# Plain float32 products in the expert layer of a fused attention and mixture-of-experts kernel

## The reference

```python
x  = L0_attn_x
xn = layernorm(x)
out = x + attention(xn, w_qkv, w_out) + ffn(xn, wg, w1, b1, w2, b2)

def ffn(...):                      # 8 experts, 2 of them for each token
    xt = xn.reshape(8192, 256)
    scores = softmax(xt @ wg); topv, topi = top_k(scores, 2)
    # each expert takes 2048 tokens (capacity), others are dropped
    disp = zeros(8, 2048, 256) with the chosen tokens' rows at their slots
    h = relu(einsum("ecm,emh->ech", disp, w1) + b1)     # w1: 8 x 256 x 1024
    y = einsum("ech,ehm->ecm", h, w2) + b2              # w2: 8 x 1024 x 256
    out = sum over the 2 choices of gate * y[expert, slot]
```

## Time and profile before

| | |
|---|---|
| median of the runs | 3241.0 us |
| time of the profiled execution | 3247.3 us |
| its span on the core | 3245.3 us |
| TensorE busy | 3037.0 us, 94% |
| TensorE weight loads busy | 2426.4 us |
| VectorE busy | 2254.5 us, 69% |
| ScalarE busy | 1674.7 us, 52% |
| GpSimd busy | 1612.6 us, 50% |

### The profile page before, as it was taken

How to read it: one execution, slowest core, us unless ns; L and a number is a source line. 1 busy time by engine, 2 the same in 40 slices (tenths; PEclk the granted TensorE clock), 3 DMA queues, 4 the chain that set the end, 5 groups by cost and what they waited for, 6 DMA issues and landing times.

```text
span 3245.3 us, 64713 instructions
## 1 busy us (share of the span) xinstructions
PE 3037.0 (94%) x22677; PEld 2426.4 (75%) x22677; DVE 2254.5 (69%) x5152; ACT 1674.7 (52%) x3798; POOL 1612.6 (50%) x2384
## 2 busy tenths in 40 slices
PE   5589999999989999999999999999999999999996
PEld 3479998999977777777777777777777777777774
DVE  6844444444347778778877877787788778777875
ACT  2444444444445555555555555555555555555553
POOL 2132221222136665666566566656665665666563
PEclk7799999999999999999999999999999999999999
DMA  6022221222123323333233333333332333333232
GB/s 207 32 78 75 72 72 56 65 74 77 51 63 78 96 76 100 89 87 105 73 100 78 100 80 94 100 79 92 85 100 73 100 97 84 83 90 98 70 90 71
DMA packets 205201, 274.70 MB, mean 85 GB/s; under 512 B 61520, under 2 KB 161872, under 8 KB 204896
## 3 DMA queue, kind: packets, MB, share of 16 engines
q1 hardware_dynamic: 180288, 203.51, 22.6%
q0 software_dynamic: 24608, 67.17, 7.7%
HBM read 102.80 MB, written 33.55 MB: 42 GB/s over the span
## 4 chain that ended last, share of the span: by engine, by line
PE 55%; ACT 6%; DVE 5%; issue 4%; SPq 1%; DMA 0%; DVEq 0%
PE S L1272 14%; PE O L1309 13%; PE S L1188 8%; PE T L1285 8%; ACT pr L1347 4%; PE W L1223 3%; PE S L1203 3%; PE W L1203 3%; PE W L1188 3%; DVE pr L1404 2%; DVE kl L1435 1%; ACT kh L1362 1%; DVE ol L1449 1%; SPq L1125 1%; ACT oh L1372 1%
## 5 line engine op out<-in xcount | busy, mean ns | idle before, releaser
L1347 ACT ACTIVATE pr<-pr,negm 128x128 f32<-128x128 f32 (+7 forms) x1024 | 787.2, 770 | 756.5 <-DVE negm L1404 755.3
L1549 POOL TENSOR_SCALAR pr<-pr,rinv 128x128 f32<-128x128 f32 (+7 forms) x1024 | 759.6, 749 | 828.8 <-DVE rinv L1410 821.4
L1404 DVE CUSTOM_DVE_ANT_0 pr<-S,late 128x128 f32<-128x128 f32 (+7 forms) x1024 | 731.0, 751 | 48.1 <-PE S L1272 40.5
L1309 PE MATMUL O<-pT,vv 128*64 128x256 f32 (+1 forms) x5120 | 558.0, 364 | 14.0 <-DMA pT<-squares 13.2
L1309 PEld LDWEIGHTS O<-pT,vv 128*64 128x64 f32 x5120 | 345.7, 137 | 203.8 <-issue 24.1
L1339 DVE COPY pT<-T 128x512 f32<-128x512 f32 (+3 forms) x704 | 364.1, 540 | 147.3 <-PE O L1309 147.3
L1285 PE MATMUL T<-ident,pr 128*128 128x128 f32 x2688 | 420.6, 281 | 19.2 <-DVE pT L1339 18.6
L886 DVE TENSOR_TENSOR hl<-h,hh 128x512 fp32r<-128x512 f32 x256 | 191.5, 748 | 317.7 <-ACT hh L847 310.6
L1285 PEld LDWEIGHTS T<-ident,pr 128*128 128x128 f32 x2688 | 295.8, 140 | 133.5 <-issue 95.5
L843 ACT ACTIVATE h<-pH,b1c 128x512 f32<-128x512 f32 x256 | 175.9, 687 | 366.9 <-PE pH L773 353.0
L1272 PE MATMUL S<-kh,qh 64*128 64x512 f32 (+2 forms) x1536 | 319.6, 407 | 39.0 <-DVE negm L1404 34.9
(11 more groups left out here) (186 smaller groups left out, 6543.5 us busy)
## 6 DMA issues: line engine op xcount, KB each, us to landing
pT<-squares SPq DMA_DIRECT2D x768, 128.0 KB
pT<-squares POOLq DMA_DIRECT2D x256, 128.0 KB
y<-yb SPq DMA_DIRECT2D x128, 128.0 KB, 1.7
wr<-in_L_attn_w_qkv SPq DMA_DIRECT2D x128, 128.0 KB, 2.3
x<-in_L_attn_x SPq DMA_DIRECT2D x16, 512.0 KB, 5.4
xn<-xn SPq DMA_DIRECT2D x16, 512.0 KB, 5.1
w1r<-in_L_ffn_w SPq DMA_DIRECT2D x8, 1024.0 KB
w2r<-in_L_ffn_w SPq DMA_DIRECT2D x8, 1024.0 KB
```

Of the source, the lines that this page charges most:

```text
L1309: ins = e.matmul(O[hs, a:GQ], vv[n // 2 % 2][:, kt, vs], turned_p, start=(kt == 0), stop=(kt == KT - 1))
L1347: e.activation(pr[i][:, 0:w], pr[i][:, 0:w], ACT.Exp, bias=negm[:, i:i + 1], scale=-1.0, accum_out=rsum[:, i:i + 1]).then_inc(expd.sem, 1)
L1404: e.tensor_tensor_reduce(pr[i][:, 0:w], S[s % 2][:, off:off + w], late[:, SEQ - w:], 1.0, -MASKED, ALU.add, ALU.min, negm[:, i:i + 1]).the ...
L1549: e.tensor_scalar(pr[i][:, 0:width(s)], pr[i][:, 0:width(s)], rinv[:, i:i + 1], 1.0, ALU.mult, ALU.mult).then_inc(scaled.sem, 1)
```

## The change

The experts' tiles become plain float32: `xT` in place of `xh` and `xl`, `w1` and `w2` (two buffers each, which the DMA fills) in place of raw, high and low parts, `hT` in place of `h`, `hh` and `hl`. Each product of both projections is one `matmul` of float32 tiles in place of three of float32r tiles. The row copies move from ScalarE to VectorE, ScalarE writes `hT` straight from `pH`, all splitting of weights goes. SyncE now issues the loads of an expert's weights after the four stores of the group, not before them. The buffers `yb` move to an allocation that lasts over the next stage.

```diff
 def route(...):
             e.activation(ex[:]...., w[:]...., ACT.Exp).then_inc(s_exp, 1)
-            round_first(e)
             e.wait_ge(s_iota, 2)
...
 def experts(...):
-        xh = two(lambda i: sb(f"xh{i}", [P, MC, GS], F32R))
-        xl = two(lambda i: sb(f"xl{i}", [P, MC, GS], F32R))
+        xT = two(lambda i: sb(f"xT{i}", [P, MC, GS]))
...
-        h32 = two(lambda i: sb(f"h32_{i}", [P, GS]))
-        hh = two(lambda i: sb(f"hh{i}", [P, HC, GS], F32R))
-        hl = two(lambda i: sb(f"hl{i}", [P, HC, GS], F32R))
-        yb = [sb(f"yb{i}", [P, MODEL]) for i in range(GT)]
+        hT = two(lambda i: sb(f"hT{i}", [P, HC, GS]))
+        yb = start_of_next.yb
...
         @block.sync
-                        if g == 0 and not (last and par == 1):
-                            e.wait_ge(wlo.sem, wlo.at(x, 2))
-                            if first and par == 0:
...
-                            load_w(x + 1, 1 - par)
...
                             e.dma_start(row(yv_d, ...), yb[t][:]).then_inc(yst[t].sem, 16)
+
+                        if g == 0 and not (last and par == 1):
+                            apart(e, s_apart[1])
+                            load_w(x + 1, 1 - par)
...
         @block.gpsimd
-                        if g == 1 and not (last and par == 1):
-                            e.wait_ge(fY.sem, fY.at(sg - 1, 0))
-                            split(x + 1, 1 - par)
...
         @block.tensor
             def up(sg, par, q, hc, first):
                 if hc == 0:
-                    e.wait_ge(xhi.sem, xhi.at(sg, 1))
-                    e.wait_ge(xlo.sem, xlo.at(sg, 1))
+                    e.wait_ge(xt.sem, xt.at(sg, 1))
...
-                terms = [(w1h, xh), (w1h, xl), (w1l, xh)]
-                n = 0
                 for m in range(MC):
-                    for w, xx in terms:
-                        ins = e.matmul(pH[hc % 4][:], w[par][:, m, ws], xx[q][:, m, :], start=(n == 0), stop=(n == 3 * MC - 1))
-                        n += 1
+                    ins = e.matmul(pH[hc % 4][:], w1[par][:, m, ws], xT[q][:, m, :], start=(m == 0), stop=(m == MC - 1))
                 ins.then_inc(fH.sem, 1)
 
             def down(sg, par, q, t, first):
                 if t == 0:
-                    e.wait_ge(hlo.sem, hlo.at(sg, HC))
+                    e.wait_ge(rl.sem, rl.at(sg, HC))
...
                 for hc in range(HC):
-                    for n, (hs, ws) in enumerate(((hh, w2h), (hh, w2l), (hl, w2h))):
-                        ins = e.matmul(pY[t % 2][:], hs[q][:, hc, ts_], ws[par][:, hc, :],
-                                       start=(hc == 0 and n == 0), stop=(hc == HC - 1 and n == 2))
+                    ins = e.matmul(pY[t % 2][:], hT[q][:, hc, ts_], w2[par][:, hc, :], start=(hc == 0), stop=(hc == HC - 1))
...
         @block.scalar
-                            e.activation(h32[hc % 2][:], pH[hc % 4][:], ACT.Relu, bias=b1c[par][:, hc:hc + 1]).then_inc(rl.sem, 1)
...
-                            e.activation(hh[q][:, hc, :], h32[hc % 2][:], ACT.Copy).then_inc(hhi.sem, 1)
...
+                            e.activation(hT[q][:, hc, :], pH[hc % 4][:], ACT.Relu, bias=b1c[par][:, hc:hc + 1]).then_inc(rl.sem, 1)
...
         @block.vector
             def rows(sg, q, first=False):
+                e.wait_ge(tX.sem, tX.at(sg, 1))
+                if not first:
+                    e.wait_ge(fH.sem, fH.at(sg - 2, HC))
                 for m in range(MC):
-                    ins = e.tensor_tensor(xl[q][:, m, :], pX[m][:], xh[q][:, m, :].bitcast(F32), ALU.subtract)
-                ins.then_inc(xlo.sem, 1)
+                    ins = e.tensor_copy(xT[q][:, m, :], pX[m][:])
+                ins.then_inc(xt.sem, 1)
...
-                            e.tensor_tensor(hl[q][:, hc, :], h32[hc % 2][:], hh[q][:, hc, :].bitcast(F32),
-                                            ALU.subtract).then_inc(hlo.sem, 1)
```

More of the change, by code:

```diff
@@ L323, in _, with route @@
             turn(UNITS - 1, 1, False)
-def route(nc, k, logits, pick, slot_token, prefetch, biases, round_first):
+def route(nc, k, logits, pick, slot_token, prefetch, biases):
     E = EXPERTS
@@ L541, in biases @@
                              bass.IndirectOffsetOnAxis(ap=t["rows"][0:EXPERTS * HC, 0:1], axis=0)).then_inc(t["s_b1"], 16)
-    return t, first, biases, round_first
+    return t, first, biases
 class Start:
@@ L573, in __init__ @@
         self.s_xn = [sem(f"s_start_xn{i}") for i in range(len(self.pr))]
+        self.yb = [sb(f"yb{i}", [P, MODEL]) for i in range(4)]
         self.s_yst = [sem(f"s_yst{i}") for i in range(4)]
@@ L680, in body @@
                         sg, q = PER * x + g, g % 2
-                        if g == 0 and not (last and par == 1):
-                            e.wait_ge(wlo.sem, wlo.at(x, 2))
-                            if first and par == 0:
+                        if first and par == 0 and g == 0:
+                            for b in range(2):
                                 apart(e, s_apart[1])
[L685 to L692, removed]
+                                e.wait_ge(gat[b].sem, gat[b].at(0, 16 * GT))
                             apart(e, s_apart[1])
-                            load_w(x + 1, 1 - par)
+                            e.wait_ge(fH.sem, fH.at(0, 1))
                         if last and par == 1 and g == 1:
@@ L723, in gather @@
                                          bass.IndirectOffsetOnAxis(ap=idx[q][:, t:t + 1], axis=0)).then_inc(gat[q].sem, 16)
[L725 to L730, removed]
             gather(0, 0, 0, True)
@@ L754, in rows @@
                 if not first:
[L755 to L756 removed]
+                    e.wait_ge(xt.sem, xt.at(sg - 1, 1))
                 for m in range(MC):
@@ L817, in _ @@
         def _(e):
[L818 to L824, removed]
             e.wait_ge(s_b1t, 1)
             e.activation(b1T[:], pY[0][:, 0:EXPERTS * HC], ACT.Copy).then_inc(s_b1c0, 1)
-            rows(0, 0, True)
             def body(i, first, last):
@@ L837, in body @@
                         sg, q = PER * x + g, g % 2
-                        start = first and par == 0 and g == 0
                         for hc in range(HC):
                             e.wait_ge(fH.sem, fH.at(sg, hc + 1))
-                            if not (start and hc < 2):
-                                e.wait_ge(hlo.sem, hlo.at(sg, hc - 1))
-                            e.activation(h32[hc % 2][:], pH[hc % 4][:], ACT.Relu, bias=b1c[par][:, hc:hc + 1]).then_inc(rl.sem, 1)
-                            e.wait_ge(rl.sem, rl.at(sg, hc + 1))
                             if hc == 0 and not (first and par == 0 and g < 2):
                                 e.wait_ge(fY.sem, fY.at(sg - 2, GT))
-                            e.activation(hh[q][:, hc, :], h32[hc % 2][:], ACT.Copy).then_inc(hhi.sem, 1)
-                            if hc == 2 and not (last and par == 1 and g == PER - 1):
-                                rows(sg + 1, (g + 1) % 2, start)
+                            e.activation(hT[q][:, hc, :], pH[hc % 4][:], ACT.Relu, bias=b1c[par][:, hc:hc + 1]).then_inc(rl.sem, 1)
             loop(e, body)
@@ L854, in _, with rows @@
         def _(e):
-            def rows(sg, q):
-                e.wait_ge(xhi.sem, xhi.at(sg, 1))
+            def rows(sg, q, first=False):
+                e.wait_ge(tX.sem, tX.at(sg, 1))
+                if not first:
+                    e.wait_ge(fH.sem, fH.at(sg - 2, HC))
                 for m in range(MC):
-                    ins = e.tensor_tensor(xl[q][:, m, :], pX[m][:], xh[q][:, m, :].bitcast(F32), ALU.subtract)
-                ins.then_inc(xlo.sem, 1)
-            def split(x, q, j):
-                raw, hi, lo = ((w1r, w1h[q], w1l[q]), (w2r, w2h[q], w2l[q]))[j]
-                e.wait_ge(whi.sem, whi.at(x, j + 1))
-                e.tensor_tensor(lo[:], raw[:], hi[:].bitcast(F32), ALU.subtract).then_inc(wlo.sem, 1)
+                    ins = e.tensor_copy(xT[q][:, m, :], pX[m][:])
+                ins.then_inc(xt.sem, 1)
             def down(sg, par, t, first):
@@ L872, in down @@
                 e.tensor_tensor(yb[t][:], pY[t % 2][:], b2c[par][:], ALU.add).then_inc(yv.sem, 1)
-            split(0, 0, 0)
-            split(0, 0, 1)
-            rows(0, 0)
+            rows(0, 0, True)
             def body(i, first, last):
@@ L884, in body @@
                         for hc in range(HC):
-                            e.wait_ge(hhi.sem, hhi.at(sg, hc + 1))
-                            e.tensor_tensor(hl[q][:, hc, :], h32[hc % 2][:], hh[q][:, hc, :].bitcast(F32),
-                                            ALU.subtract).then_inc(hlo.sem, 1)
                             if hc == 2 and not (last and par == 1 and g == PER - 1):
-                                rows(sg + 1, (g + 1) % 2)
+                                rows(sg + 1, (g + 1) % 2, start)
                             if hc % 2 and not start:
```

(4 more changed lines are left out.)

42 lines of the change are left out of this document (15 added, 27 removed).

## The result

The changed kernel takes 3403.43 us (median of two runs, 3402.16 to 3404.69), against 3241.0 before: ratio 1.0501 with a 95% interval of 1.0456 to 1.0546. It is 5.0% slower, 162 us. The forecast was 3398 us in a range of 3385 to 3460 us. The profiled execution took 3402.2 us with a span of 3400.3.

The account below looks back on a forecast made before the run. TensorE's product time was taken to bound the experts' stage; products +160.7, start -1.1 and stall -2.8 us summed to +156.8 us on the median of 3241.0, giving 3398 us, range 3385 to 3460 us.

Parts of the forecast that it names:

- What bounds: Experts' products stretch, 752.6 us: only TensorE's product time counts; less work on other engines is worth nothing except where TensorE waited.
- Price of a float32 record: Experts' products: each float32 product is two records, 0.427 us each for 512 columns, 0.217 for 256; +160.7 us.
- The upper bound from the whole round: One attention round of float32 products, start and handover included: at most 0.227 us for a record of 256 columns.
- Products before: Experts' float32r products in the kernel before: 1536 x 0.232 plus 3072 x 0.1188, 721 us in all.
- The second way to 721: Experts' stretch of 752.6 us less 4.4 us of standing still and 27 us of transposes leaves 721 us.
- The stall: TensorE's 2.8 us wait before the first down product goes, as the split and `hl` go: -2.8 us.
- Start: Start of the experts' stage: rows go through VectorE alone, first product 1.1 us earlier; between 0 and -2 us.
- The split of the first weights: VectorE's work at the stage's start, said to be hidden by the 10.7 us wait for the gather: gives nothing.
- The first: Rival: in the experts' stage a float32 product costs only two float32r products, 481 us replacing 721; 2997 us, chance 0.03.
- the rule of the Trainium skill: Matrix engine peak "÷2 for FP32_LOW_HIGH": for the whole product a gain, for each of two records in agreement with the trace.
- The second rival: Experts' float32 products keep float32r's pace for each column pass, 0.464 us per 512-column record; 3478 us, chance 0.06.
- The third and fourth: Rivals: tiles go through as one float32r record, 2757 us, chance 0.01; TensorE waits once a group, 3430 us, chance 0.05.

Follow-up runs that it names:

- the two halves of the change: The kernel before with only the up products in plain float32, ratio 1.0258, and with only the down products in plain float32, ratio 1.0247.
- The experiment with the later rounding: The kernel before, with GpSimd's rounding of an expert's weights waiting for one down tile more: 3238.11 us, ratio 0.9987.
- The idle subtractions: The kernel after the change with two idle 128 x 2048 subtractions on VectorE at the start of the experts' stage: 3403.24 us.

## Why the prediction was right

- **What bounds.** Shown. With 218 us less of VectorE's work and 188 us less of ScalarE's in the stretch, the time followed TensorE's products alone, and the two halves of the change added up.
- **Price of a float32 record.** 0.427 us was taken, 0.4288 measured for 512 columns; 0.217 taken, 0.2156 measured for 256. The attention's 0.2156 us is the very number of the new down products: whether 64 columns of weights or 128 makes no difference. Up 437 forecast and 439 measured, down 444 and 442, together 881.6 and 881. The upper bound from the whole round, 0.227 us, was not reached in any group; that a start and a handover made it so is argued, not shown.
- **Products before.** 721 us was 4 us too much. Its paces come from one of the dearest groups; on the mean of eight, (23.27 - 0.88) x 32 = 717 us. The second way to 721 agreed only because it left out that TensorE ran at a granted clock of 0.50 (the 1.2 GHz level) from 169.6 to 173.4 us and from 190.5 to 193.5, which cost 1.8 and 1.4 us. So the products grew by 164 us, not by 160.7.
- **The stall.** The 2.8 us went as forecast, and 1.4 us at the lower clock behind it went too, which the prediction did not count. The experiment with the later rounding shows both. A wait of 1.9 us for issue stands in place of 1.6. The first twelve records took 7.84 us (162.98 to 170.82) in place of 5.1, which is 0.9 us more lost at the lower clock than at the same place before. Together: 164 - 2.8 - 1.4 + 0.3 + 0.9 = 161 us, by which the stretch grew; 157.9 were forecast for it.
- **Start.** -1.1 us for the row copies, as forecast. The split of the first weights was put at nothing, since the wait for the gather covered it. That step was wrong, by 3.0 us: the cover was itself lengthened by the work that it was to hide. The idle subtractions gave back 1.7 of them through the gathers, the one subtraction left in each half of the change 1.8, mostly through the copy. The 2.5 us ahead of the stage are chance.
- **The number.** 3398 forecast, 3403 measured. The two profiled executions differ by 154.9 us, 2 less than the forecast 156.8, the medians by 162.4: the profiled execution of before lay 6 us over its median. That the sum comes within 2 us is partly luck, since 5.5 us too little were taken off at the start (3.0 and 2.5) and 3 us too little were put on in the stretch of the products. The price of the float32 records, which makes the loss, does not hang on this.
- **Rivals.** The first (a float32 product at the price of two float32r ones) needed a record of 256 columns under 0.178 us; full weights and one product at a time give 0.2156. There were two ways to read the rule of the Trainium skill, Perfetto Trace Analysis, section Engine Utilization, and the one for each record is the one that the runs bear out: a record of 256 columns takes 0.2156 us where a bfloat16 one takes 0.109, and there are two records. The second rival, float32r's pace in each pass, would have shown 0.464 us; it was measured at 0.4288, and the run with bfloat16 parts, same shapes and order, shows that the slower pace comes with float32r and not with a full array. The third and fourth didn't occur: two records a product, and no wait in the groups.

## What to carry to other kernels

A plain float32 product costs two records, each with twice its columns in time: against three float32r products of its parts it loses even though two thirds of the instructions and all splitting go, and the sum can be made beforehand from any float32 product already in the trace, by the distance of starts at two widths. Take the price of what goes from many groups and not from one: here the one read was 0.6% too dear, 4 us. A short stall can cost more than its length: here 2.8 us of standing still had 1.4 us at the lower clock behind them. Before replacing parts by something exact and slower, ask whether the low parts are needed: one float32r product of rounded factors took the stretch from 753 to 275 us. And when the main engine becomes three times faster, look for waits in in-order queues beside it (here GpSimd's for the weights, ahead of a gather) that were free until then.

## What the runs showed of the hardware

- Float32r products start 0.232 us (512 columns) and 0.119 us (256) apart in the dearest groups, bfloat16 ones 0.217 and 0.109 us, at a granted clock of 1.00 in both. A group of float32r products takes 23.05 to 23.46 us, one of bfloat16 parts 21.71 and one of float32 products 28.42, both alike in every group but for one wait for issue. Why float32r pays some 7% more, and not the same in all groups, was not tried.
- A two-input operation of VectorE on SBUF and work of GpSimd hold each other up: GpSimd's indirect DMA took 2.20 us in place of 0.95 and a copy of 4 values a partition 1.97 in place of 0.18 under VectorE's subtraction, and a 0.69 us subtraction took 1.75 us under GpSimd's rounding. The Trainium skill, SBUF — State Buffer, section "SBUF: two separate sides", says that the two engines share a pair of ports under an exclusive lock, and that a VectorE operation with two inputs in SBUF takes it against a GpSimd operation that reads SBUF; whoever starts first holds it for the whole instruction. The traces agree with it: in the run with only the up products in float32 the subtraction ends at 158.45 us and the held copy at 158.50, and in the run with idle subtractions the copy that started 0.01 us ahead of VectorE took 0.18 us.
